# Graph attention over 8192 nodes: six tiles instead of five packed while the projection runs, the added packs behind its groups 29 and 31

## What is computed

```python
s1, s2 = h @ attn[:256, 0], h @ attn[256:, 0]
e = leaky_relu(s1[:, None] + s2[None, :], 0.2)
e = where(adj > 0, e, -9e15)
y = x + elu(softmax(e, axis=1) @ h)
out = (y - mean(y)) / sqrt(var(y) + 1e-5)      # by row
```

## Time and profile before

| | us |
|---|---|
| median of 3 runs (lowest, highest) | 843.47 (842.3, 843.72) |
| the profiled execution | 842.7 |
| its span, first to last instruction | 841.0 |
| granted TensorE clock, mean | 0.872 of 2.4 GHz |

### The profile page before, as it was taken

The page is one execution under the profiler, slowest core; times in us unless marked ns, Lnnn a source line. Parts: engine busy times, 40 slices in busy tenths (PEclk is TensorE's granted clock), DMA queues, the critical chain, the costliest instruction groups (busy, mean ns, idle before and its releaser), DMA issues.

```text
span 841.0 us, 10651 instructions
## 1 busy us (share of the span) xinstructions
PE 603.0 (72%) x2585; PEld 389.0 (46%) x2628; DVE 631.1 (75%) x2422; ACT 573.1 (68%) x529; POOL 608.5 (72%) x689
## 2 busy tenths in 40 slices
PE   6589976568776796787867766687658685776761
PEld 4467763235353463554544433445335353553431
DVE  5567653569789888789887598678868776988794
ACT  0055537569869787878787598678869776897710
POOL 4478426778788878777865788888878786887871
PEclk9699999689989998979899798799888897998975
DMA  8999996999999999999999999999999998999711
GB/s 326 403 403 423 423 410 254 417 394 407 414 411 400 396 416 415 415 415 394 408 397 422 401 376 412 404 339 362 416 420 404 414 416 302 404 415 416 289 31 45
DMA packets 61697, 316.00 MB, mean 376 GB/s; under 512 B 19158, under 2 KB 37815, under 8 KB 45248
## 3 DMA queue, kind: packets, MB, share of 16 engines
q1 hardware_dynamic: 36176, 285.49, 83.0%
q0 software_dynamic: 25456, 29.79, 10.7%
HBM read 340.59 MB, written 17.14 MB: 425 GB/s over the span
## 4 chain that ended last, share of the span: by engine, by line
issue 26%; POOL 24%; DMA 22%; DVE 18%; PE 7%; ACT 1%; POOLq 1%; SPq 0%; DVEq 0%; ACTq 0%
POOL GATH L1548 17%; DMA GATH<-haug,ids 5%; DMA WORK<-in_adj_dram,smalls 5%; DMA ADJ<-in_adj_dram 4%; DMA haug<-GATH 4%; POOL GATH L1517 4%; DMA X<-in_x_dram 3%; PE acc L550 3%; PE pk L539 2%; DVE diag L880 2%; DVE smalls L821 1%; DVE PART L890 1%; PE spare L616 1%; DVE Y L925 1%; DVE Y L908 1%
## 5 line engine op out<-in xcount | busy, mean ns | idle before, releaser
L1548 POOL DMA_INDIRECT GATH<-haug,ids x448 | 475.4, 1061 | 131.7 <-issue 128.6
L1368 ACT ACTIVATE WORK<-ADJ 128x4096 bf16<-128x4096 int32 x126 | 454.6, 3609 | 102.5 <-PE pk L539 68.1
L539 PE MATMUL pk<-WORK,D 128*128 128x512 bf16 x981 | 261.8, 416 | 121.4 <-ACT WORK L1368 117.4
L539 PEld LDWEIGHTS pk<-WORK,D 128*128 128x128 bf16 x1024 | 100.4, 104 | 259.7 <-ACT WORK L1368 144.0
L550 PE MATMUL acc<-GATH,diag 128*128 128x256 f32 x512 | 155.3, 458 | 64.7 <-DVE diag L880 64.7
L550 PEld LDWEIGHTS acc<-GATH,diag 128*128 128x128 f32 x512 | 117.0, 234 | 107.7 <-DVE diag L880 83.2
L781 DVE MAX8 smalls<-pk 128x8 f32<-128x512 f32 x64 | 44.5, 695 | 31.9 <-issue 31.9
L890 DVE SCALAR_TENSOR_TENSOR PART<-GATH,smalls,PART 128x256 f32<-128x256 f32 x128 | 62.2, 486 | 4.5
L616 PE MATMUL spare<-X,WORK 128*128 128x256 f32 x256 | 58.9, 384 | 0.0
L1521 POOL DMA_DIRECT2D haug<-GATH x32 | 23.5, 735 | 45.4 <-DVE GATH L772 45.1
L616 PEld LDWEIGHTS spare<-X,WORK 128*128 128x128 f32 x256 | 49.5, 193 | 7.1
(11 more groups left out here) (177 smaller groups left out, 807.1 us busy)
## 6 DMA issues: line engine op xcount, KB each, us to landing
ADJ<-in_adj_dram SPq DMA_DIRECT2D x128, 2048.0 KB, 15.5
haug<-GATH POOLq DMA_DIRECT2D x32, 258.0 KB, 10.5
out_dram<-Y SPq DMA_DIRECT2D x32, 256.0 KB, 9.0
GATH<-haug,ids POOLq DMA_INDIRECT x448
X<-in_x_dram SPq DMA_DIRECT2D x1, 4096.0 KB, 30.7
X<-in_x_dram SPq DMA_DIRECT2D x1, 3072.0 KB, 26.6
X<-in_x_dram SPq DMA_DIRECT2D x1, 1024.0 KB, 6.9
Waug<-in_L_gnn_W_dram SPq DMA_DIRECT2D x1, 256.0 KB, 2.7
```

What stands on the lines that cost most here:

```text
L539: done = nc.tensor.matmul(pk[s % PKS][:], D16[:, k, :], A16[:, q % 2, k * BW:(k + 1) * BW], start=(half == 0 and k == 0), stop=(half == 1 ...
L1368: act.activation(A16[:, q % 2, :], ADJ[:, q % 4, :], ACT.Relu, scale=HALF_SCALE if q % 2 else 1.0, accum_out=degree[:, q // 2, q % 2:q % 2 ...
L1548: pool.indirect_dma_start(out=GATH[:, r, k * DA:(k + 1) * DA], out_offset=None, in_=haug, in_offset=bass.IndirectOffsetOnAxis(ap=ids[:, t ...
```

## The change

```diff
-EARLY = 5
+EARLY = 6
...
-            return 5 + 3 * x if x < MC else 34 + 3 * (x - MC)
+            return 6 + 3 * x if x < MC else 34 + 3 * (x - MC)
...
-        PACK_AFTER = [8, 10, 13, 15, 17, 19, 21, 23, 25, 27]
+        PACK_AFTER = [8, 10, 12, 14, 16, 18, 21, 23, 25, 27, 29, 31]
...
             def mid_mark(k):
                 dve.wait_ge(mid_rank_steps, 2)
+                dve.wait_ge(mid_unpacked, 4 * MC)
```

## The result

| | before | after |
|---|---|---|
| median, us | 843.72 (5 runs, 842.3 to 845.28) | 848.9 (5 runs, 844.8 to 850.52) |
| after / before | | 1.0055, 95% interval 1.0031 to 1.0079 |
| span of the profiled execution | 841.0 | 847.1 |

The ratio puts the cost of the change at 4.6 us, between 2.6 and 6.7.

What follows compares the result with a forecast made beforehand. POOL, 99% full, was taken to set the end from 445 on: 8.3 us late less its 6.85 us wait gave +1.5, all else 0. On the 843.47 median that made 844.97, say 844.9; range 840.0 to 848.0.

Steps and rivals of the forecast that it cites:

- What bounds the kernel: POOL, 99% full from its first gather at 131.88, waits 6.85 us at the list's gate; from 445 the end follows POOL.
- The sum's one term: At the list's gate: POOL 8.3 us later, less its 6.85 us wait, moves the end by +1.5 us (-0.6 to +3.3).
- the later clock: At 445.26 POOL and the adjacency chain through DVE meet; whichever is later sets the end, forecast to be POOL.
- Two packs moved up: PE at the projection's end: two packs of 2.3 us, mostly hidden, delay the s2 transpose by 0 to 0.4 us.
- What they release: Adjacency stream: count 12 at about 120, gap at 127 moved to about 150, chain gains about 3 us (0 to 7.4).
- What the filled gap costs: Last h store and s2 row meet a full stream; POOL's first gate moves to 139.4, +8.3 us (6.3 to 10.1).
- The rest: Remaining effects, each priced at 0, including DVE made late by gathers 8 us later: 0 (0 to 3).
- The reserve of four halves: Adjacency stream: up to four halves in hand, 20 us, claimed to cover DVE's lateness from later gathers.
- rival C: Gathers and DVE both late: s2 row at 141.2, stream stands up to 3 us more; 846.8 to 849.8, chance 0.14.
- six signs for the forecast: DMA share in 124:140 and 148:158, count 12's time, last store's landing, POOL's first gate, list's gate wait under 1 us.
- The moved chunks: Round 0's chunks one step later: same instructions, first chunk's 1.1 us penalty moves to a later count; 0 (-1 to +1).

Runs made afterwards that it cites:

- e1: Kernel before with only round 0's chunks one step later and the added DVE wait: 842.6 us, ratio 0.9984.
- e11: Kernel before with tile 0's softmax one step later: 857.42 us, ratio 1.0156.
- e4: Kernel before with seven additions on POOL ahead of its first gather, making it 8.7 us late: 848.24 us, ratio 1.0053.
- e2: Changed kernel with round 0's chunks back in their old steps, so only the packs are moved: 845.24 us, ratio 1.0019.
- e12: Changed kernel with the counts of halves 16 and 17 moved ahead of tile 0's soft_exp on ACT: 849.52 us, ratio 1.0055.
- e5: Changed kernel run again, unaltered, in a second set of runs: 848.04 us, ratio 1.0061.
- e3: Changed kernel with half 16 asked for only when the stores of h, mean row and s2 row have landed: 839.46 us, ratio 0.9952.
- e8: e3 with half 18 also held until tile 0's seven gathers have landed: 840.17 us, ratio 0.9961.
- e6: Kernel before with three additions on POOL ahead of its first gather, making it 4.7 us late: 843.04 us, ratio 0.9997.

## Why the prediction was wrong

**What bounds the kernel: half right.** POOL is full from its first gather on, and its lateness is passed on as forecast: 9.6 us at the first gate, 7.1 at the list's, 2.5 us made up on the way. The sum's one term, +1.5 us, needs POOL to be the later clock at the list's gate. It was not: it still waited there, 8.67 us, for a list that the forecast had at 445.26 or up to 3 us earlier and that came at 454.17. That the later clock decides the end is not shown by the runs, and e1, whose gate was 4.0 us late at no cost, speaks against it.

**Two packs moved up: right.** DVE's copy of group 31 moved by 0.9 us (126.52 against 125.64), still waiting 3.00 us for a store. The mean's matmul moved from 126.53 to 127.41, and the s2 row went out 1.6 us later (130.57), where I had at most 0.4. Most of that difference may be chance: without the moved packs it goes out as late as 130.60 (e11).

**What they release: right in place, and in size only if the gathers were not later.** Count 12 began at 118.64 (forecast about 120), and half 20 was asked for at 157.3 (156 to 157). The new gap was forecast at 150 to 157 and stood at 148 to 160. I took the adjacency chain to gain 3 us. Between two kernels with POOL equally late the packs do give back 3.4 us of idle time (e4 to e2). But the late gathers take more from the same chain, 6.0 us of idle time in e4, so in the changed kernel it lost: from 7.4 to 11.0 us over 120 to 300. I had counted the gain in the stream and not the loss. e12 shows the limit: with a late first gate, a gap that is filled ahead of the gathers opens again behind them.

**What the filled gap costs: right in mechanism, low in size.** The first gate came at 140.63, inside the bounds of 137.4 to 141.2, and in e5's profile at 143.28, outside them. The last store was issued 0.9 us later than before, at 127.59, and landed after 12.0 us, where I had 12.2. The s2 row landed some 0.8 us behind it, where I had 0.5. e3 shows the mechanism: the same packs, with the stream held, start POOL at 133 and are faster than before. The rule that the Trainium skill gives in "DMA: Bandwidth & Descriptors", section "Queues, rings and completion order", that each DMA engine takes turns between the queues that have work, fits e3 and e8 as well: stores and gathers both land sooner when the stream is silent.

**The rest: here is the step that failed.** "Gathers later by 8 us can make DVE late ... four halves in hand, 20 us, which covers it: 0 (0 to 3)." In e4, with nothing of the change in it, a gather 8.7 us late cost 4.5 us. There too POOL was never the later clock: it waited 4.35 us at the list's gate for a list 4.5 us late. So what I had priced at 1.5 us through POOL cost nothing at that gate, and what I had priced at 0 through DVE was the cost.

The reserve of four halves is not there at this stage. In the kernel before, loads asked for from 135 to 175 landed after 8.0 to 14.5 us. At 5 us a half that is an estimate of two to three in flight, while from 300 on they took 14.2 to 20.0 us. ACT waited 0.6 us for loads in 140:260 and 18.4 in 300:440, so until then the compute engines are the later ones. I could have read that ahead. It fits that e6's 4.7 us were absorbed and 8.7 were not, but no run tests it.

I had priced this mechanism as rival C, 846.8 to 849.8 with 14 in 100, and the result lies in it. C's signs are in the profile, DVE waiting for gathers (though in 230:440 only at tiles 8 and 22) and a DMA share of 0.87 at 240:260. Its number is partly luck: 3.3 us of it were POOL's own lateness, which cost nothing at the gate, and the larger part of the new idle time, 5.8 us, lies at tile 0. Of my six signs for the forecast five came, and only the last failed, the wait at the list's gate under 1 us. The range ended at 848.0, in C's middle.

**The moved chunks: 0 (-1 to +1) was right alone** (-1.0 us in e1) and wrong beside late gathers, by the 3 us that stay open above. This is the second term that failed. Together: +4.5 for the late gathers (e4), -2.9 for the packs (e2 against e4), +3.0 for the chunks beside them (the changed kernel against e2) make the 4.6 measured, by the way they are taken. Each of the three is a difference with an interval of 2 us or more to either side.

## What to carry to other kernels

A gap in a saturated stream may be carrying traffic that is short of latency rather than of bandwidth. Before filling it, list the small transfers that land in it and what starts on their landing; here holding the stream for a few us until they were in turned a loss of 4.6 us into a gain of 4.0. And when a transfer is released earlier, follow what gates the ones after it: if that is a computation fed by the same DMA engines, the gap moves instead of closing. And a reserve that is there late in a run need not be there at its start: read the landing times of the loads in the stage in question (here 8.0 to 14.5 us early, 14.2 to 20.0 us late).

## What the runs showed of the hardware

A 32 KB row store that takes 1.8 us on idle DMA engines (before, e3) took 9.8 and 11.8 us on a full stream (changed kernel, e5), and a 258 KB store 12.0 instead of 2.8 us. The seven gathers of a tile, 128 rows each, landed 4.8 us after the last issue with the next loads held back (e8), and 9.8 us after it with them running (e3). Beside POOL's additions on 128x512 float32 a DVE TENSOR_SCALAR on 128x8 took 1.00 us instead of 0.15 (e4).
